# Three programs between attention stages made one, and score tiles of the third cross stage sent in whole pairs

## Chip, cores and metric
The kernel runs on one core of a Trainium2 chip. The metric is the device time of one execution in microseconds (us), the median of several runs; lower is better.

## What is computed
A transformer of four layers over x of 8 batches x 256 tokens x 128 channels (16 heads of 8), with a context of 8 x 1601 tokens and one conditioning vector per batch. Layers 0 to 2 have the same outline; the norms, gates and score masks differ:

```
mod = act(cond) @ W_mod + b_mod                    # shift, scale, gate per batch
h = norm(x) * (1 + scale) + shift
x = x + gate * proj(self_attention(q, k, v of h))    # 256 keys; layer 1 rotary, layer 2 windows of 64
x = x + gate * proj(cross_attention(q of h', k and v of ctx))   # 1601 keys; layer 2 keeps the top 16 scores
x = x + gate * mlp(norm(x) * (1 + scale) + shift)    # 128 -> 512 -> 128; layer 2 gated
```

Layer 3 is a cross attention with one head, whose result goes with the normed x into three routed experts and a gate.

## The kernel before, in words
Activations lie transposed, channels on the 128 partitions: `p.x` and `p.o_all` hold 2048 tokens as columns, worked on in NC = 4 chunks of CH = 512 columns. Queries and keys are split in three bf16 parts each (so products keep float32's precision), written to DRAM (`store_q`, `store_k`, three DMAs each, runs of 1 KB) and read back per batch in stacked form (`q_st`, `k_st`; two DMAs each, runs of 512 B).

Each stage is a `nc.Block()` of its own: five programs (TensorE PE, VectorE DVE, ScalarE ACT, GpSimd POOL, SyncE SP, which issues all DMAs), with a barrier at its end. `program` calls, for each layer, `stage_load` (weights and vectors by DMA, then the modulation: 6 or 9 matmuls, `p.modv`), `stage_project` (`Norm`, then keys, queries and values; splits by VectorE and GpSimd; stores), `stage_attention` self (in whose tail `Onward` makes the cross queries), `stage_attention` cross and `stage_mlp` (`OutProj`, `Norm`, up and down matmuls). Layer 2's cross attention is `stage_last`, which has mixed into it the layer's MLP, and layer 3's attention; then come `stage_load(3)` and `stage_experts`.

`Norm` goes breadth first: mean of all four chunks, then variance, then a matmul that spreads 1/std (`diag`), then scale and shift on ScalarE. `stage_mlp` uses two PSUM banks for up (L1463) and one for down (L1450); after the last residual (L1492 or L1490, and L1496) the block ends. `stage_load` then loads the weights (L189). `stage_project` makes the projections (L556) and values (L564), splits (L596 to L608), and stores queries and keys (L157, L164) and values (L532) in the order q0 k0 q1 k1 q2 q3 v v k2 v v k3. In the self attention SP first loads masks (layer 2 only, L1029, L1030), then queries, keys and values of batches 0 and 1 (L1036, L1043, L1048); after a zero matmul (L1133) the first score (L1156) waits for the keys.

Within attention stages a planner (`Plan`) sets a fixed order. A step k is one tile of 128 keys of one unit n (a unit is a batch b and a group of 4 heads, 32 in all; 13 steps per unit in cross attention, NT = 13). In each step TensorE makes `x_scores(k)`, items of the ring of PSUM banks, and `values` for a step before. The ring carries score tiles ("s": 128 queries of one head x about 400 keys; NS = 32 tiles per unit), turned maxima ("m"), projections of the next batch's context ("k", "v") and in `stage_last` the side items of `LastOrder` (co, mean, var, bc, m1a, m1b, m2, q3, k3, v3, s3, t3, x3, rb at steps counted from `first(b)`, here called d). How many score tiles have been sent by the end of step k is

```
upto = min(NU * self.NS + (turn if beside else 0), ((k + 1) * self.NS // NT + lead) // 2 * 2)
```

In `stage_last` (BANKS = 3, four rows `s_sb` of 1601 scores) ScalarE copies each score tile to `s_sb` (L2004). One such row holds a head's scores of 128 queries, 4 tiles; a pair is two of them, 8 tiles. VectorE finds the 16 largest of each row in 8 operations per pair (MAX8, MATCH_REPLACE8, L2283 to L2292), which are counted in `g["chain"]`, 8 per pair just as the tiles. Before its row can be filled with the scores of two pairs later, ScalarE makes `un` of it (`mark`, L1995), which `x_scores` uses to leave out all but the 16 largest. VectorE's side work for step k (`between(k)`: co and m2 L2214, mean L2219, var L2221, bc L2223, m1b L2227, s3 L2230) is put in the chain at

```
def slot(k):
    return (k + 1) * NS // NT + LEAD - 10        # LEAD = HQ * NCH + 16 = 48
```

Of the kernel before, what the change touches and what calls it, by code (L numbers as in the profile page):

```python
# [7 lines left out]
F32 = mybir.dt.float32  # L8
# [96 lines left out]
class Program:  # L105
    def __init__(self, nc, ctx, io):
# [12 lines left out]
        self.vec = self.sb("vec", [P, V_MAX])  # L119
        self.modv = self.sb("modv", [P, 9, B])  # L120
# [5 lines left out]
        self.v_dram = dram("v_dram", (B, P, 2, NH * VW), F32)  # L126
# [44 lines left out]
def vector(p, layer, name, n=0):  # L171
    at = V_OFF[layer][0][name] + n
    return p.vec[:, at:at + 1]


def stage_load(p, layer):

    nc, (w_off, n_w), (v_off, n_v) = p.nc, W_OFF[layer], V_OFF[layer]
    loaded, act_ready, mm_ready, mod_ready, rows_set = (p.sig(s) for s in ("w_loaded", "cact_ready", "mod_mm", "mod_ready", "rows_set"))
    n_mod = dict(L_WEIGHTS[layer]).get("mod", 0)  # L180
    n_dma = 2 + (5 if layer == 0 else 0)
    scale_slots = [] if layer == 3 else [m[layer][0] for m in (MOD_SELF, MOD_CROSS, MOD_MLP) if m[layer][0] is not None]
    with ExitStack() as ctx:
        mod_ps = p.ps(f"mod_ps{layer}", [P, 9, B], ctx)
        block = ctx.enter_context(nc.Block())

        @block.sync
        def _(sp):
            sp.dma_start(p.w[:, 0:n_w, :], p.io[f"w{layer}"]).then_inc(loaded.sem, 16)  # L189
            sp.dma_start(p.vec[:, 0:n_v], p.io[f"v{layer}"]).then_inc(loaded.sem, 16)  # L190
            if layer == 0:
                sp.dma_start(p.cond[:], p.io["cond"]).then_inc(loaded.sem, 16)
                sp.dma_start(p.const[:], p.io["const"]).then_inc(loaded.sem, 16)
                sp.dma_start(p.neg_id[:], p.io["neg_id"]).then_inc(loaded.sem, 16)
                sp.dma_start(p.id_bf[:], p.io["id_bf"]).then_inc(loaded.sem, 16)
                sp.dma_start(p.x[:], p.io["x"]).then_inc(loaded.sem, 16)
            sp.wait_ge(loaded.sem, loaded.at(16 * n_dma))

        if layer == 0:
            @block.gpsimd  # L200
            def _(pool):
                for hf in range(2):
                    nc.gpsimd.memset(p.q_st[64 * hf + 32:64 * hf + 64], 0.0).then_inc(rows_set.sem, 1)
                pool.wait_ge(rows_set.sem, rows_set.at(2))

        if n_mod:
            @block.scalar
            def _(act):
                act.wait_ge(loaded.sem, loaded.at(16 * n_dma))

                nc.scalar.activation(p.cact[:], p.cond[:], ACT.Copy if layer == 1 else ACT.Silu).then_inc(act_ready.sem, 1)

            @block.tensor
            def _(pe):
                pe.wait_ge(loaded.sem, loaded.at(16 * n_dma))
                pe.wait_ge(act_ready.sem, act_ready.at(1))
                for s in range(n_mod):
                    last = nc.tensor.matmul(mod_ps[:, s, :], weight(p, layer, "mod", s), p.cact[:], start=True, stop=True)
                last.then_inc(mm_ready.sem, 1)

            @block.vector
            def _(dve):
                if layer == 0:
                    for hf in range(2):
                        nc.vector.memset(p.k_flat[64 * hf + 32:64 * hf + 64], -1.0)
                dve.wait_ge(mm_ready.sem, mm_ready.at(1))
                bias = p.vec[:, v_off["mod"]:v_off["mod"] + n_mod]
                nc.vector.tensor_tensor(p.modv[:, 0:n_mod, :], mod_ps[:, 0:n_mod, :],
                                        bias[:, :, None].to_broadcast([P, n_mod, B]), ALU.add).then_inc(mod_ready.sem, 1)
                dve.wait_ge(mod_ready.sem, mod_ready.at(1))  # L230
                for s in scale_slots:
                    last = nc.vector.tensor_scalar(p.modv[:, s, :], p.modv[:, s, :], 1.0, None, ALU.add)
                last.then_inc(mod_ready.sem, 1)
    loaded.passed(16 * n_dma)
    if n_mod:
        act_ready.passed(1)
        mm_ready.passed(1)
        mod_ready.passed(2)
# [96 lines left out]
class Norm:  # L335
# [4 lines left out]


    def __init__(self, p, ctx, layer, scale, shift):
        self.p, self.layer, self.scale, self.shift = p, layer, scale, shift
        self.xc = p.sb("n_xc", [P, NC, CH], F32, ctx)
        self.sq = p.sb("n_sq", [P, NC, CH], F32, ctx)
        self.diag = p.sb("n_diag", [P, NC, CH], F32, ctx)
        self.h = p.sb("n_h", [P, NC, CH], F32, ctx)
        self.rv = p.sb("n_rv", [P, NC, 4], F32, ctx)
        self.rstd = p.sb("n_rstd", [P, NC, 4], F32, ctx)
        self.mean_ps = p.ps("n_mean", [P, NC, CH], ctx)  # L350
        self.var_ps = self.mean_ps[:, :, 0:4]
# [73 lines left out]
def mod_slot(p, layer, slot):  # L425
    if slot is None:
        return lambda b: None
# [2149 lines left out]
```

## Time and profile before

| | |
|---|---|
| three runs, median (lowest to highest) | 4625.27 us (4620.71 to 4640.73) |
| the profiled execution, its time | 4624.74 us |
| its span, first to last instruction | 4623.0 us |
| PE busy | 3625.3 us, 78% |
| PEld (weight loads) busy | 1609.1 us, 35% |
| DVE busy | 3536.7 us, 77% |
| ACT busy | 2945.9 us, 64% |
| POOL busy | 691.4 us, 15% |
| moved by DMA | 280.05 MB |
| mean granted TensorE clock | 0.80 |

Times in the profile are us from the span's start. A row of the timeline gives start, duration, engine, line, operation, output and inputs, how many instructions were merged, and in brackets the idle time of the engine before it with what ended it. In a row of windows the numbers in brackets are instructions. The order of the engines in a row of windows is PE, PEld, DVE, ACT, POOL. A DMA share can come out a little above 1. In front of a row with SPq the engine only issues; the transfer comes after.

### The profile page before, as it was taken

The numbers are of one execution on the slowest core, as the hardware profiler recorded it, in microseconds if no ns is written. First come the engines' busy times: TensorE is split into PE (matmuls) and PEld (weight loads), VectorE is DVE, ScalarE is ACT, GpSimd is POOL, SyncE is SP. The second block draws the span as 40 slices with busy tenths as digits, with TensorE's granted clock in tenths as the row PEclk, the third lists the DMA queues.
The fourth block names the chain that finished last, engine by engine and source line by source line (L and its number), as shares of the span: only waits on it lengthen the run. The fifth ranks groups of instructions, "written<-read, shape, count | busy, mean of one in ns | idle before, by whom it ended". The sixth has DMA issues, their size and how long they took to land. (4 is left out here: it accounts for less than half of the span.)

```text
span 4623.0 us, 75349 instructions
## 1 busy us (share of the span) xinstructions
PE 3625.3 (78%) x28388; PEld 1609.1 (35%) x28388; DVE 3536.7 (77%) x5424; ACT 2945.9 (64%) x5480; POOL 691.4 (15%) x1464
## 2 busy tenths in 40 slices
PE   2769999976789999858367778787787878778877
PEld 2323333332323333323132334334343434334543
DVE  7658989826568888537699998898989889898213
ACT  1556888844647878627377776767677677766413
POOL 1322122004234242013011010000101000000000
PEclk7788999987879999878666677777777667766769
DMA  4553353205434333144311011110111011000000
GB/s 138 147 132 85 85 112 84 57 22 144 120 91 95 90 94 80 24 107 118 80 36 43 22 29 37 31 34 19 40 30 37 18 32 34 13 12 10 13 19 9
DMA packets 277795, 280.05 MB, mean 61 GB/s; under 512 B 38960, under 2 KB 252472, under 8 KB 276536
## 3 DMA queue, kind: packets, MB, share of 16 engines
q1 hardware_dynamic: 277432, 275.22, 23.9%
q8 instruction: 226, 3.70, 0.4%
q14 instruction: 137, 1.12, 0.1%
HBM read 149.53 MB, written 124.43 MB: 59 GB/s over the span
## 5 line engine op out<-in xcount | busy, mean ns | idle before, releaser
L1369 DVE TENSOR_REDUCE mpart<-ring 128x1 f32<-128x400 f32 (+2 forms) x2816 | 1293.0, 524 | 273.9 <-PE ring L1156 267.1
L1287 ACT ACTIVATE prob<-xa_ps 128x512 f32<-128x512 f32 (+1 forms) x2048 | 1109.8, 596 | 243.5 <-PE xa_ps L1201 223.1
L2068 ACT ACTIVATE prob<-x_ps 128x512 f32<-128x512 f32 (+1 forms) x832 | 451.9, 598 | 313.3 <-PE x_ps L1926 246.5
L1156 PE MATMUL ring<-k_st,q_st 52*128 52x400 bf16 (+2 forms) x2560 | 580.7, 340 | 43.2 <-DMA k_st<-k_dram 11.3
L1790 PE MATMUL ring<-k_st,q_st 52*128 52x400 bf16 (+1 forms) x1024 | 330.5, 444 | 294.2 <-ACT s_sb L2004 276.3
L1220 PE MATMUL xa_ps<-prob,va 128*9 128x256 f32 x6656 | 506.4, 383 | 0.4 <-ACT prob L1287 0.4
L2283 DVE MAX8 mpart<-s_sb 128x8 f32<-128x1601 f32 x256 | 456.1, 1817 | 61.5 <-ACT s_sb L2004 61.5
L2004 ACT ACTIVATE s_sb<-ring 128x400 f32<-128x400 f32 (+1 forms) x1024 | 468.2, 517 | 40.1 <-PE ring L1790 31.8
L1995 ACT ACTIVATE un<-s_sb 128x1601 fp8e4<-128x1601 f32 x256 | 392.9, 1536 | 128.8 <-DVE s_sb L2292 128.3
L2286 DVE MATCH_REPLACE8 s_sb<-mpart,s_sb 128x1601 f32<-128x1601 f32 x256 | 461.9, 1812 | 0.0
L2292 DVE MATCH_REPLACE8 s_sb<-m8b,s_sb 128x1601 f32<-128x1601 f32 x256 | 461.8, 1812 | 0.0
L2289 DVE MAX8 m8b<-s_sb 128x8 f32<-128x1601 f32 x256 | 454.6, 1816 | 0.0
L1201 PE MATMUL xa_ps<-q_st,k_st 55*128 55x256 bf16 (+1 forms) x3840 | 408.6, 279 | 56.7 <-ACT prob L1287 43.5
L1921 PE MATMUL x_ps<-neg_id,un 128*128 128x128 bf16 (+1 forms) x3328 | 349.9, 268 | 47.0 <-ACT prob L2068 46.1
L1921 PEld LDWEIGHTS x_ps<-neg_id,un 128*128 128x128 fp8e4 (+1 forms) x3328 | 286.3, 128 | 188.6 <-ACT prob L2068 131.0
L1943 PE MATMUL av_ps<-prob,va 128*9 128x256 f32 (+1 forms) x3328 | 338.2, 496 | 0.0
L1156 PEld LDWEIGHTS ring<-k_st,q_st 52*128 52x128 bf16 x2560 | 180.1, 95 | 408.5 <-DVE mpart L1369 259.6
L1790 PEld LDWEIGHTS ring<-k_st,q_st 52*128 52x128 bf16 x1024 | 84.8, 112 | 511.8 <-ACT s_sb L2004 387.3
L1201 PEld LDWEIGHTS xa_ps<-q_st,k_st 55*128 55x128 bf16 (+1 forms) x3840 | 142.3, 96 | 314.1 <-ACT prob L1287 287.4
L1926 PE MATMUL x_ps<-q_st,k_st 55*128 55x256 bf16 (+1 forms) x1664 | 210.1, 342 | 0.0
L1271 ACT ACTIVATE mT<-ring 24x128 bf16<-24x128 bf16 x160 | 41.9, 262 | 211.9 <-PE ring L1162 210.3
L1220 PEld LDWEIGHTS xa_ps<-prob,va 128*9 128x9 f32 x6656 | 105.3, 88 | 188.8 <-issue 108.2
(291 smaller groups left out, 4195.3 us busy)
## 6 DMA issues: line engine op xcount, KB each, us to landing
k_st<-kc_dram SPq DMA_DIRECT2D x192, 300.2 KB, 5.5
o_dram<-o_sb SPq DMA_DIRECT2D x192, 128.0 KB, 1.8
kc_dram<-k SPq DMA_DIRECT2D x72, 300.0 KB, 3.4
ctx_t<-in_ctxT SPq DMA_DIRECT2D x24, 800.5 KB, 4.8
q_st<-q_dram SPq DMA_DIRECT2D x80, 192.0 KB, 4.2
kc_dram<-k SPq DMA_DIRECT2D x72, 200.0 KB, 3.9
k_st<-k_dram SPq DMA_DIRECT2D x48, 192.0 KB, 5.0
kc_dram<-k SPq DMA_DIRECT2D x24, 300.8 KB, 3.3
```

What stands on the lines that cost most here:

```text
L1156: nc.tensor.matmul(ring_ps[:, r % BANKS, 0:w], q_st[rows, b % NQ, 2 * t + pl, qt * P:(qt + 1) * P], k_st[rows, slot_of(n), pl, c0:c0 + w], ...
L1201: last = nc.tensor.matmul(x_ps[0:sizes[j], (2 * s + hf) % XBANKS, pl * T:(pl + 1) * T], k_st[rows, slot_of(n), pl, keys], q_st[rows, b % N ...
L1220: last = nc.tensor.matmul(av_ps[32 * k:32 * k + VW, n % 2, :], va[0:sizes[j], b % NVB, j, G * t + k, :], prob[0:sizes[j], s % NPROB, (2 * ...
L1287: nc.scalar.activation(prob[0:size, s % NPROB, hf * 512:(hf + 1) * 512], x_ps[0:size, (2 * s + hf) % XBANKS, :], ACT.Exp, scale=HEAD_SCALE ...
L1369: nc.vector.tensor_reduce(mpart[:, n % 4, row, c:c + 1], ring_ps[:, r % BANKS, 0:chunks[c][1]], AX.X, ALU.max).then_inc(g["red"].sem, 1)
L1921: nc.tensor.matmul(x_ps[0:sizes[j], (2 * s + hf) % XBANKS, pq * P:(pq + 1) * P], un[:, n % 2, hf * G + pq, keys], p.neg_id[:], start=pq == ...
L2004: nc.scalar.activation(s_sb[:, q % 4, c0:c0 + w], ring_ps[:, r % BANKS, 0:w], ACT.Copy).then_inc(g["rout"].sem, 1)
L2068: nc.scalar.activation(prob[0:size, s % NPROB, hf * 512:(hf + 1) * 512], x_ps[0:size, (2 * s + hf) % XBANKS, :], ACT.Exp, scale=HEAD_SCALE ...
L2283: ins = nc.vector.max(best, sc)
L2286: ins = nc.vector.match_replace(sc, best, sc, -BIG)
L2289: ins = nc.vector.max(m8b[:, half, :], sc)
L2292: ins = nc.vector.match_replace(sc, m8b[:, half, :], sc, -BIG)
```

## The change
- `stage_load` is called once, for layer 0. `stage_project` and `stage_mlp`, with `OutProj` and `Norm`, are replaced by `stage_between` (class `Between`), called ahead of each self attention: for layer 0 with norm and projections alone, for layers 1 and 2 from the output projection of the cross attention before through the MLP to the new layer's projections, in one block.
- Its SP program loads the next layer's weights up to the place of `co` at the start, the rest after the last down matmul. `p.vec` and `p.modv` have two sets. Next modulation: matmuls between norm and up.
- PSUM use is a rotation of four banks for all products and four for statistics.
- Values go straight to SBUF (`vs`) and stay for all batches; `v_dram` goes, and so do the loads of values.
- Queries and keys of batches 0 and 1 are loaded within the stage, in front of its last three stores; layer 2's masks at its start. The order of stores is q0 k0 q1 k1 q2, loads, q3 k2 k3.
- In `Plan`, with `beside` (only `stage_last`), the number of tiles sent is rounded down to whole pairs, 8; LEAD is 52; VectorE's side work goes behind the second operation of the last pair sent.
- The one zero matmul of 512 columns in `stage_last` becomes two of 256.

```diff
-def stage_load(p, layer):
+def stage_load(p):
...
-            sp.dma_start(p.w[:, 0:n_w, :], p.io[f"w{layer}"]).then_inc(loaded.sem, 16)
+            sp.dma_start(p.w[:, 0:W_OFF[0][1], :], p.io["w0"]).then_inc(loaded.sem, 16)
...
+class Between:
...
+    HEAD = ("op", "mean", "var", "diag", "norm", "mod", "up", "down")
+    TAIL = ("mean", "var", "diag", "norm", "proj")
+    NF = 4
...
+        self.by_pool = [("k", c) for c in range(NC - 1)]
+        self.by_dve = [("q", c) for c in range(NC)] + [("k", NC - 1)]
...
+    def out(self, use):
+        return self.bank[:, self.at[use] % 4, :]
...
+        def bank_free(use):
+            u = self.at[use]
+            if u == 3 and self.layer is not None:
+                pe.wait_ge(s["bias"].sem, s["bias"].at(1))
+            if u >= 4:
+                old = self.uses[u - 4]
+                read = s[self.reader(old)]
+                pe.wait_ge(read.sem, read.at(self.nth[old]))
...
+            elif k == "mod" and c == 0:
+                pe.wait_ge(s["w"].sem, s["w"].at(32))
+                bank_free(("mod", 0))
+                act_in = p.cond if self.nxt == 1 else p.cact
+                for i in range(self.n_mod):
+                    last = nc.tensor.matmul(self.out(("mod", 0))[:, i * B:(i + 1) * B], weight(p, self.nxt, "mod", i), act_in[:], start=True, stop=True)
+                last.then_inc(s["mm"].sem, 1)
+            elif k == "up":
+                pe.wait_ge(s["h"].sem, s["h"].at(2 * n + 2))
+                for f in range(self.NF):
+                    use = (("up", f), c)
+                    bank_free(use)
+                    nc.tensor.matmul(self.out(use), weight(p, self.layer, "m1", f), self.h[:, c, :], start=True, stop=True).then_inc(s["mm"].sem, 1)
+            elif k == "down":
+                pe.wait_ge(s["act"].sem, s["act"].at(self.nth[("up", self.NF - 1), c]))
+                bank_free(("down", c))
+                for f in range(self.NF):
+                    last = nc.tensor.matmul(self.out(("down", c)), weight(p, self.layer, "m2", f), self.hid[:, c, f, :], start=f == 0, stop=f == self.NF - 1)
+                last.then_inc(s["mm"].sem, 1)
...
+            elif k == "proj":
+                pe.wait_ge(s["h"].sem, s["h"].at(2 * n + 2))
+                for name in self.names:
+                    use = (name, c)
+                    bank_free(use)
+                    if name == "v":
+                        for i in range(4):
+                            last = nc.tensor.matmul(self.out(use)[:, i * P:(i + 1) * P], self.h[:, c, i * P:(i + 1) * P], weight(p, self.nxt, "v"), start=True, stop=True)
+                    else:
+                        last = nc.tensor.matmul(self.out(use), weight(p, self.nxt, name), self.h[:, c, :], start=True, stop=True)
+                    last.then_inc(s["mm"].sem, 1)
+
...
+                    if name == "v":
+                        if c == 0:
+                            act.wait_ge(s["ones"].sem, s["ones"].at(1))
+                        dst = self.vs[:, 2 * c:2 * c + 2].rearrange("p b j h w -> p (b j) h w")[:, :, :, 0:HD]
+                        nc.scalar.activation(dst, self.out(use).rearrange("p (k h d) -> p k h d", k=4, d=HD), ACT.Copy).then_inc(s["act"].sem, 1)
+                        continue
...
+            if k in ("op", "down"):
+                self.residual(dve, c, k)
...
+            elif k == "proj" and c == 0:
+                for what, chunk in self.by_dve:
+                    done = self.split(dve, nc.vector, s["dchain"], done, what, chunk, s["dparts"])
+
...
+    def pool(self, pool):
+        self.p.nc.gpsimd.memset(self.vs[:], 1.0).then_inc(self.s["ones"].sem, 1)
+        done = 0
+        for what, c in self.by_pool:
+            done = self.split(pool, self.p.nc.gpsimd, self.s["pchain"], done, what, c, self.s["pparts"])
...
+        p, s, nxt = self.p, self.s, self.nxt
+        if self.layer is not None:
+            n_w, free = W_OFF[nxt][1], W_OFF[self.layer][0]["co"]
+            sp.dma_start(p.w[:, 0:free, :], p.io[f"w{nxt}"][:, 0:free, :]).then_inc(s["w"].sem, 16)
+            sp.dma_start(p.vec[:, nxt % 2, 0:V_OFF[nxt][1]], p.io[f"v{nxt}"]).then_inc(s["w"].sem, 16)
+        if self.rope:
+            sp.dma_start(self.table[:], p.io["rope"][:, :, 0:T]).then_inc(s["tab"].sem, 16)
+        if nxt == 2:
+            for hf in range(2):
+                rows = slice(64 * hf + STACK, 64 * hf + STACK + MASK_ROWS)
+                for par in range(NQ):
+                    sp.dma_start(self.q_self[rows, par], p.io["qmask"][:, None, :].to_broadcast([MASK_ROWS, NH // 2, T])).then_inc(s["init"].sem, 16)
+                keys = p.k_flat[rows, 0:NQ * NH // 2 * T].rearrange("r (n c) -> r n c", c=T)
+                sp.dma_start(keys, p.io["kmask"][:, None, :].to_broadcast([MASK_ROWS, NQ * NH // 2, T])).then_inc(s["init"].sem, 16)
+        if self.layer is not None:
+            sp.wait_ge(s["mm"].sem, s["mm"].at(self.at["down", NC - 1] + 1))
+            sp.dma_start(p.w[:, free:n_w, :], p.io[f"w{nxt}"][:, free:n_w, :]).then_inc(s["w2"].sem, 16)
+
+        def store(what, c):
+            mine, ready = (self.by_pool, s["pparts"]) if (what, c) in self.by_pool else (self.by_dve, s["dparts"])
+            sp.wait_ge(ready.sem, ready.at(mine.index((what, c)) + 1))
+            cols, st = slice(c * CH, (c + 1) * CH), s["st" if c else "st0"]
+            if what == "q":
+                store_q(sp, p.q_dram, cols, self.parts[:, c, 0], st)
+            else:
+                store_k(sp, p.k_dram, cols, self.parts[:, c, 1], st)
+
+        for what, c in (("q", 0), ("k", 0), ("q", 1), ("k", 1), ("q", 2)):
+            store(what, c)
+        sp.wait_ge(s["st0"].sem, s["st0"].at(32 * len(RUNS)))
+        for b in range(Q_AHEAD):
+            load_queries(p, sp, self.q_self, b, s["loaded"])
+            load_keys(p, sp, b, s["loaded"])
+        for what, c in (("q", 3), ("k", 2), ("k", 3)):
+            store(what, c)
+        for name in ("loaded", "st", "w", "w2", "init"):
+            if self.totals[name]:
+                sp.wait_ge(s[name].sem, s[name].at(self.totals[name]))
...
-        self.ring, self.items = [], {}
+        self.ring, self.items, self.upto = [], {}, {}
+        whole = 2 * NCH if beside else 2
         self.at, self.nth, self.n_act, self.n_dve = {}, {}, 0, 0
...
-            upto = min(NU * self.NS + (turn if beside else 0), ((k + 1) * self.NS // NT + lead) // 2 * 2)
+            self.upto[k] = upto = min(NU * self.NS + (turn if beside else 0), ((k + 1) * self.NS // NT + lead) // whole * whole)
...
-        va = p.va if cross else p.sb("va_self", [P, NVB, NT, NH, VW], F32, ctx)
+        va, NVB = (p.va, 2) if cross else (vs, B)
...
-            for b in bload_at.get(-1, []):
-                load_q(b)
-                load_k_self(b)
-                load_v(b)
...
-    LEAD = HQ * NCH + 16
+    LEAD = HQ * NCH + 20
...
-            nc.tensor.matmul(av_ps[:].rearrange("p u c -> p (u c)"), zero[:, 0:P], zero[:], start=True, stop=True)
+            for u in range(2):
+                nc.tensor.matmul(av_ps[:, u, :], zero[:, 0:P], zero[:], start=True, stop=True)
...
-                return (k + 1) * NS // NT + LEAD - 10
+                return plan.upto[k] - 2 * NCH + 2
...
-            stage_load(p, layer)
-            if layer == 0:
-                stage_context_norm(p)
-            stage_project(p, layer)
-            stage_attention(p, layer, "self")
+            with ExitStack() as mid:
+                vs = p.sb("vs", [P, B, 2, NH, VW], F32, mid)
+                q_self = p.sb("q_masked", [P, NQ, NH // 2, T], BF16, mid) if layer == 2 else p.q_st
+                stage_between(p, layer - 1 if layer else None, layer, vs, q_self)
+                stage_attention(p, layer, "self", vs, q_self)
             if layer < 2:
                 stage_attention(p, layer, "cross")
-                stage_mlp(p, layer)
         with ExitStack() as last:
             nx = p.sb("nx3", [P, TOK], F32, last)
             stage_last(p, nx)
-            stage_load(p, 3)
+            stage_load_last(p)
```

## Rows read from the trace of the kernel before

**Rows 1.** Timeline, layer 0 to 1 (start us, us, engine, line, operation, [idle before])
```profile
965.02 0.69 DVE L474 TENSOR_TENSOR x<-x,op_res 128x512 f32<-128x512 f32 x1
...
978.12 1.88 PE L1463 MATMUL ml_ps<-n_h,w 128*128 128x512 f32 x4
...
1006.85 3.67 PE L1450 MATMUL ml_ps<-ml_hid,w 128*128 128x512 f32 x8 [1.26 <-DVE ml_res L1492]
...
1011.66 0.69 DVE L1496 TENSOR_TENSOR x<-x,ml_res 128x512 f32<-128x512 f32 x1
...
1039.93 14.10 PE L556 MATMUL pj_ps<-n_h,w 128*128 128x512 f32 x32
...
1044.47 3.43 DVE L596 TENSOR_TENSOR pj_f<-pj_f,pj_table 128x512 f32<-128x512 f32 x2 [3.65 <-ACT pj_f L576]
...
1080.43 0.69 DVE L608 TENSOR_TENSOR pj_q<-pj_f,pj_q 128x512 bf16<-128x512 f32 x1
...
1095.46 0.61 PE L1156 MATMUL ring<-k_st,q_st 52*128 52x256 bf16 x4 [5.65 <-DMA k_st<-k_dram]
```

**Rows 2.** Timeline, layer 1 to 2
```profile
1962.13 1.88 PE L1463 MATMUL ml_ps<-n_h,w 128*128 128x512 f32 x4
...
2006.16 3.98 PE L218 MATMUL mod_ps<-cact,w 128*128 128x8 f32 x18 [10.08 <-ACT cact L211]
...
2026.48 7.39 PE L556 MATMUL pj_ps<-n_h,w 128*128 128x512 f32 x16
...
2034.13 1.58 SPq L157 DMA_DIRECT2D q_dram<-pj_q  x3
...
2057.59 1.32 SPq L1029 DMA_DIRECT2D q_masked<-in_qmask  x4
...
2073.79 0.61 PE L1156 MATMUL ring<-k_st,q_masked 52*128 52x256 bf16 x4 [15.15 <-DMA k_st<-k_dram]
```

**Rows 3.** Timeline, projections of layer 0 to its first score
```profile
136.37 1.56 SPq L157 DMA_DIRECT2D q_dram<-pj_q  x3
...
160.56 0.60 PE L1133 MATMUL xa_ps<-zero 1*128 1x512 bf16 x1 [20.88 <-DVE zero L1357]
...
166.84 0.61 PE L1156 MATMUL ring<-k_st,q_st 52*128 52x256 bf16 x4 [5.68 <-DMA k_st<-k_dram]
```

**Rows 4.** Timeline of VectorE, first two pairs of the third cross stage
```profile
2252.50 3.56 DVE L2283 MAX8 mpart<-s_sb 128x8 f32<-128x1601 f32 x2 [3.27 <-ACT s_sb L2004]
...
2266.60 3.55 DVE L2283 MAX8 mpart<-s_sb 128x8 f32<-128x1601 f32 x2
```

**Rows 5.** Window before side work starts: us, busy per engine, PEclk, DMA share, GB/s
```profile
2300.00:2600.00 300.00, 205.85 (x1543) 89.12 (x1545) 300.00 (x258) 213.37 (x368) 26.95 (x52) 0.67 0.13 36
```

**Rows 6.** Waits of VectorE, 2250 to 4290 us (us in total, times, longest)
```profile
DVE mpart L2283 <- ACT s_sb L2004: 61.5, 15, 10.4
...
DVE ls_res L2214 <- PE ring L1837: 35.7, 12, 6.5
...
DVE ls_xc L2223 <- PE ring L1837: 14.5, 11, 1.6
...
DVE ls_xc L2219 <- PE ring L1837: 13.9, 8, 2.5
...
DVE ls_mpart L2230 <- PE ring L1853: 13.0, 14, 1.7
...
DVE ls_rv L2221 <- PE ring L1844: 10.8, 7, 1.7
```

**Rows 7.** Windows: layer 0's stores, then its loads
```profile
148.00:152.00 4.00, 0.00 (x0) 0.00 (x0) 1.98 (x4) 0.00 (x0) 0.00 (x0) 0.50 1.02 349
...
164.00:166.00 2.00, 0.00 (x0) 0.00 (x0) 0.00 (x0) 0.00 (x0) 0.00 (x0) 0.50 1.19 190
```

**Rows 8.** Page, costliest groups: ScalarE's copies of scores and its marks
```profile
L2004 ACT ACTIVATE s_sb<-ring 128x400 f32<-128x400 f32 (+1 forms) x1024 | 468.2, 517 | 40.1 <-PE ring L1790 31.8
...
L1995 ACT ACTIVATE un<-s_sb 128x1601 fp8e4<-128x1601 f32 x256 | 392.9, 1536 | 128.8 <-DVE s_sb L2292 128.3
```

More of the change, by code:

```diff
@@ L197, in _ @@
-            sp.wait_ge(loaded.sem, loaded.at(16 * n_dma))
[L199 to L233, printed above, removed]
@@ new lines, in _ @@
+        @block.tensor
+        def _(pe):
+            pe.wait_ge(loaded.sem, loaded.at(16 * n_dma))
+            pe.wait_ge(act_ready.sem, act_ready.at(1))
+            for s in range(n_mod):
+                last = nc.tensor.matmul(mod_ps[:, s, :], weight(p, 0, "mod", s), p.cact[:], start=True, stop=True)
+            last.then_inc(mm_ready.sem, 1)
+        @block.vector
+        def _(dve):
+            for hf in range(2):
+                nc.vector.memset(p.k_flat[64 * hf + 32:64 * hf + 64], -1.0)
+            dve.wait_ge(mm_ready.sem, mm_ready.at(1))
+            bias = p.vec[:, 0, at:at + n_mod]
+            nc.vector.tensor_tensor(modv[:, 0:n_mod, :], mod_ps[:, 0:n_mod, :], bias[:, :, None].to_broadcast([P, n_mod, B]), ALU.add).then_inc(mod_ready.sem, 1)
+            dve.wait_ge(mod_ready.sem, mod_ready.at(1))
+            for s in scale_slots(0):
+                last = nc.vector.tensor_scalar(modv[:, s, :], modv[:, s, :], 1.0, None, ALU.add)
+            last.then_inc(mod_ready.sem, 1)
@@ L539, in _ @@
-            store_v(2)
-            store_v(3)
-            store("k", 3)
-            sp.wait_ge(stored.sem, stored.at(16 * len(RUNS) * NI))
-            sp.wait_ge(v_st.sem, v_st.at(32 * NV))
+            bt.sp(sp)
         @block.tensor
         def _(pe):
-            norm.pe(pe)
-            for i in range(NI):
-                what, c = items[i]
-                names = names_of[what]
-                norm.wait_h(pe, c)
-                for r in range(stepn):
-                    n = i * stepn + r
-                    if n >= 3:
-                        pe.wait_ge(pf.sem, pf.at(n - 2))
-                    nc.tensor.matmul(pp[:, n % 3, :], weight(p, layer, names[r]), norm.h[:, c, :], start=True, stop=True).then_inc(proj.sem, 1)
@@ L557, in _ @@
-            for g in range(NV):
-                m = NI * stepn + g
-                if g < 3:
-                    pe.wait_ge(pf.sem, pf.at(m - 2))
-                else:
-                    pe.wait_ge(v_out.sem, v_out.at(g - 2))
-                for k in range(4):
-                    last = nc.tensor.matmul(pp[:, m % 3, k * P:(k + 1) * P], norm.h[:, g, k * P:(k + 1) * P], weight(p, layer, "v"), start=True, stop=True)
-                last.then_inc(v_mm.sem, 1)
+            bt.pe(pe)
         @block.scalar
@@ L627, in stage_project @@
[L627 to L632 removed]
+            bt.pool(pool)
+    bt.done()
 class Onward:
@@ L900, in by_step, with stage_attention @@
     return out
-def stage_attention(p, layer, kind):
+def stage_attention(p, layer, kind, vs=None, q_self=None):
     nc = p.nc
     cross = kind == "cross"
-    masked = layer == 2 and not cross
     rope = layer == 1
```

641 lines of the change are left out of this document (272 added, 369 removed).

## The prediction

> **What bounds the kernel now.** I read the page first. VectorE is busy for 77% of the span, TensorE for 78% and ScalarE for 64%; no engine is full throughout, so the stages have to be taken one by one. The chain that ended last reaches back only into the experts' stage, which the change leaves alone. I then read the timeline around the three places where `stage_project` hands over to a self attention, and for the third cross stage (2247 to 4467 us) the waits and busy times of VectorE.
>
> At the hand-over between layers 0 and 1 every step is serial [rows 1]. The last residual ends at 1011.66 + 0.69 = 1012.35. Only behind it, in a program of its own, are the weights asked for and the modulation made; then the norm runs, and projection matmuls start at 1039.93. The first split of queries starts at 1044.47 and the first score at 1095.46. Layer 1 to 2 has the same shape [rows 2]. At the start of layer 0 [rows 3] only the last part is there: first store 136.37, first score 166.84.
>
> In the third cross stage VectorE's top-16 passes are the metronome: one pair of score rows (eight operations) takes 2266.60 - 2252.50 = 14.10 us [rows 4], so 128 pairs need 1805 us. They last to about 4292. Up to 2600 VectorE never idles [rows 5], but after that, once the side work of the last layer (`LastOrder`) is mixed in, it waits; the largest kinds of wait are [rows 6], 149 us together.
>
> **The change part by part, the hand-overs.**
> The order of the levels (op, mean, var, diag, norm, up, down) is what `OutProj`, `Norm` and `stage_mlp` do now, so I cost everything up to the norm at nothing. From there, layer 0 to 1:
> - The modulation's matmuls are put ahead of the MLP. 18 of them take 3.98 us [rows 2], 12 then 2.65. Their weights are asked for at the start of the stage, some 20 us earlier, and MLP work covers that.
> - Up and down are 64 TensorE instructions over 512 columns. 32 of that kind took 14.10 us [rows 1], so 64 take 28.2. Four banks in place of two take out the bank waits.
> - The last residual ends 1.8 us after the last down matmul (1012.35 - 1010.52) [rows 1].
> - The next norm: from the end of a first-half residual to the first matmul behind the norm it is 978.12 - 965.71 = 12.4 us [rows 1].
> Start of the projections: 978.12 + 2.65 + 28.2 + 1.8 + 12.4 = 1023.2 against 1039.93, a gain of 16.8. For layer 1 to 2: 1962.13 + 3.98 + 28.2 + 1.8 + 12.4 = 2008.5 against 2026.48, a gain of 18.0.
>
> From projections to scores. The 8 stores of values and the 2 loads go; queries and keys of two batches are loaded before the last three stores. This looks like much, but the DMA engines carry it. In the stores the rate is 349 GB/s, in the loads with their half as long runs 190 GB/s [rows 7]. The 24 stores of queries and keys write 6.3 MB, 18.2 us, and the 8 loads fetch 1.57 MB, 8.3 us: 26.5 us of transfers. From a first store at 136.37, with 0.7 to get going, that ends at 163.6. Now it is 7.5 MB of stores, 21.4 us, to 158.5, and the zero matmul behind the barrier ends at 161.16 [rows 3], 2.7 later. So the first score comes at 166.3 against 166.84: a gain of 0.5. The stores of values (1.18 MB, 3.4 us) are what is saved, and putting the loads ahead is worth little, because they queue on the same engines.
> If instead SP's issue were the limit, the last store would leave about 1.6 us sooner than now and the loads would cost nothing afterwards: 7 us. I take 0.5, because the share of the DMA engines in [rows 7] is full; 7 is the other end.
> The Trainium skill (DMA: Bandwidth & Descriptors, Specifications) puts line rate at runs of 512 B and up, which is just what these loads have. By that rule the loads would take 4.5 us and each hand-over would gain 3.8 us more; the trace disagrees, 190 against 349 GB/s.
>
> Layer 1 to 2 gains the same, and the masks: they are loaded ahead of the stage's work instead of between barrier and score. Now it is 2073.79 - 2034.13 = 39.7 us from the first store to the first score [rows 2]; afterwards 166.3 - 136.4 = 29.9. Gain 9.8 in all. In layer 1 the rope splits set the pace, 51.0 us from the first split to the score [rows 1]. VectorE's five splits end at 1081.12, 36.7 us in. The loads have then been at the DMA engines since the third, so the last three stores (2.36 MB, 6.8 us) run from about 39 us on, and 2.7 follow: 48.5. Gain 2.5.
> Sum: 0.5 + 16.8 + 2.5 + 18.0 + 9.8 = **48 us** (47.6). The low end is 32 (TensorE enters the MLP or the norm at the low clock, which doubles its part of a few microseconds, and the stores and loads mix badly), the high end adds 3 x 6.5: 67.
>
> **The change part by part, whole pairs.** The score tiles of a pair are now sent in one step every 3.25 steps, and VectorE reads the side results of a step behind the second operation of the last pair sent. Sending a pair needs the pair two before it to be finished, because there are four rows of `s_sb`. I count in chain operations of 1.76 us how far VectorE has gone past that point when it asks for a side result. Now it is 0 to 6: co, mean, var and the first m1b have 0 or 1, bc 2, m2 3. Afterwards it is 10 for each, 17.6 us instead of 0 to 10.6. So the waits for mean, bc, var and s3 in [rows 6] should go: 13.9 + 14.5 + 10.8 + 13.0 = **52 us**. I keep the wait for ls_res (35.7): most of it is the co at the end of the heavy stretch. The m1b waits stay also: step d+13 gets the same slot as bc of d+10, and shift, m1 and Silu must run between the two.
>
> The heavy stretch (x3 and values3, 13 steps) is limited by TensorE and ScalarE; 61.5 us of waits on s_sb are of there [rows 6]. Whole pairs give some 4 us more lead per batch, 7 x 4 = 28 us saved; against that the eight copies at 517 ns and two marks at 1536 ns [rows 8] come in one lump in which TensorE has little to do. I take these two as equal: 0. Ends: all of 61.5 + 35.7 goes (-97), or as much is added (+97).
> At the end the last batch but one's m1b is read behind the chain instead of inside it, and m2 waits for it: about one step, 14.1 / 3.25 = 4 us lost.
> Sum: 52 - 4 = **48 us**. The rest (LEAD 16 to 20, two zero matmuls for one, the second set of vectors) I cost at nothing: the stage's first burst is 48 tiles before and after.
>
> The profiled execution is 4623.0 + 1.7 around it = 4624.7, as good as the median 4625.3. Forecast: 4624.7 - 48 - 48 = **4529 us**.
>
> **The rivals.**
> 1. *The stage swallows it.* The side results come in time but VectorE waits for s_sb instead, since the round of TensorE and ScalarE is the true limit once side work is mixed in. For it: the s_sb waits are the largest single kind. Against: VectorE is full until 2600. The hand-overs' 48 alone: 4577.
> 2. *The heavy stretch is relieved as well.* The longer lead is enough. 4529 - 97 = 4432, halfway 4480.
> 3. *Slower.* Place: `x_scores` and `values` in the steps behind a lump. During eight copies and two marks (8 x 0.517 + 2 x 1.536 = 7.2 us) TensorE has eight short matmuls. The granted clock in the quiet stretch is 0.67 [rows 5], a mixture of the two levels, 1.2 and 2.4 GHz. If it fell to 0.50 throughout, its busy share of 206/300 would be 0.69 x 0.67 / 0.50 = 0.92, that is 13.0 of a pair's 14.1 us, and with 1.6 to 3.1 us of lump that TensorE can't fill 14.6 to 16.1. It decides from 48/128 = 0.4 us a pair. At 1.2 us a pair over 128 pairs, 154 us: 4577 + 154 = 4731. Against: a busier TensorE has the clock given back, and VectorE waits now in spite of small lumps, so the present order isn't better at that either.
> The Trainium skill (TensorE: Matmul & The Clock Gate, HAM oscillation) says that matmul groups with idle gaps between them are throttled again each time; that is this rival, and it would give its 4731.
> 4. *The hand-overs don't give 48*, for example because waves in one program run at the low clock or the final wait on stores hides the earlier start: 25 instead, with 48 from the stage: 4552.
>
> **How the numbers follow.** Forecast (4495 to 4560) 0.45, rival 1 0.18, rival 2 0.17, rival 3 0.12, rival 4 0.08. Under about 0.5%, 23 us, a measurement can't tell the two kernels apart. Faster by more: everything but rival 3 and a part of rival 1, 0.85; within: 0.06; slower: 0.09, since a small loss of clock would only eat the gain. The range goes from 4440, most of rival 2, to 4600, the hand-overs' 32 with 7 lost in the stage; it leaves out rival 3 and the far end of rival 2, under 2 in 10.
>
> **What would show it.** In the profile after, no weight load between the MLP and the norm; projections some 17 and 18 us sooner after the cross stage's end; first score 29 to 31 us after the first store in layers 0 and 2, with the DMA share full in between. If that is 23 us, the DMA argument is wrong. In the third stage VectorE's waits for mean, bc, var and s3 near zero, the m1b waits still there, pairs still 14.1 us apart before side work starts. If they are over 14.5 us there, or the granted clock is near 0.5, rival 3 holds; if the wait for s_sb grows by as much as the others shrink, rival 1.

## The result and the profile after

Three runs of the changed kernel took 4751.39 us (4739.22 to 4765.99) against 4625.27: a ratio of **1.0266**, 95% interval 1.0207 to 1.0326. It is **slower by about 126 us**, where 4529 was forecast. The profiled execution took 4739.22 us, its span is 4737.4, against 4623.0: 114.4 more. VectorE and ScalarE are busy as long as before: 3539.4 us (3536.7) and 2948.6 (2945.9). TensorE is busy for 3714.6 us against 3625.3, 89 more; in one stretch the same work runs at a lower clock, as shown below. Ratios here and below compare fast executions alone; one slower execution each of e6, e9 and e12 is in the median but not in the ratio.

**The hand-overs.** The timeline of after, with the rows that answer to [rows 1 to 3]:

```profile
138.19 1.56 SPq L156 DMA_DIRECT2D q_dram<-bt_parts  x3
...
169.10 0.61 PE L1217 MATMUL ring<-k_st,q_st 52*128 52x256 bf16 x4
...
969.75 0.69 DVE L569 TENSOR_TENSOR x<-x,bt_f 128x512 f32<-128x512 f32 x1
...
983.15 1.40 PE L456 MATMUL bt_bank<-cond,w 128*128 128x8 f32 x12
...
984.41 13.98 PE L463 MATMUL bt_bank<-bt_h,w 128*128 128x512 f32 x32
...
998.23 13.90 PE L468 MATMUL bt_bank<-bt_hid,w 128*128 128x512 f32 x32
...
1013.19 0.69 DVE L569 TENSOR_TENSOR x<-x,bt_f 128x512 f32<-128x512 f32 x1
...
1025.33 3.60 PE L479 MATMUL bt_bank<-bt_h,w 128*128 128x512 f32 x8
...
1078.37 0.61 PE L1217 MATMUL ring<-k_st,q_st 52*128 52x256 bf16 x4
...
1933.89 0.69 DVE L569 TENSOR_TENSOR x<-x,bt_f 128x512 f32<-128x512 f32 x1
...
1990.96 1.88 PE L479 MATMUL bt_bank<-bt_h,w 128*128 128x512 f32 x4
...
1998.60 1.58 SPq L156 DMA_DIRECT2D q_dram<-bt_parts  x3
...
2028.91 0.61 PE L1217 MATMUL ring<-k_st,q_masked 52*128 52x256 bf16 x4
```

The norm no longer waits for weights or modulation: the rest of the next layer's weights is asked for at 1012.15, beside it, and nothing there waits for them. The first score comes 17.1 us sooner in layer 1 (1095.46 - 1078.37) and 44.9 in layer 2 (2073.79 - 2028.91), but 2.3 later in layer 0. Between layer 0's stores and its first score, from 147 to 166 us, the share of the DMA engines is 1.00 to 1.25, full throughout.

**The third cross stage.** I take the starts of VectorE's 128 pairs (first MAX8 of each). The first is at 2213.1 us instead of 2252.5, 39.4 sooner; the last at 4384.7 instead of 4276.0. From first to last it is 2171.6 us instead of 2023.5, 148.1 more, and 352.7 instead of 347.0 from there to the end. -39.4 + 148.1 + 5.7 = 114.4: the whole difference.

The 148.1 are not spread evenly. The first 26 pairs are 14.1 us apart in both kernels, and the granted clock there is no lower than before: 0.69 (2260 to 2560 us) against 0.67 in [rows 5]. After that a batch of 16 pairs takes (mean of five batches, in groups of four pairs) 61.9, 62.5, **71.2**, 67.6 us before and 62.6, 64.4, **90.4**, 70.5 after. The third group is the heavy stretch, with x3 and values3; six of them hold 114 of the 148 us. Two heavy groups of before, then two of after (columns as in [rows 5]):

```profile
3104.60:3173.65 69.05, 59.07 (x429) 33.12 (x425) 57.38 (x53) 47.75 (x87) 2.87 (x7) 0.83 0.10 26
3624.93:3699.75 74.82, 68.48 (x415) 37.59 (x413) 57.47 (x52) 45.35 (x83) 2.85 (x7) 0.66 0.09 24
```

```profile
2807.34:2901.66 94.32, 80.43 (x418) 42.62 (x419) 57.41 (x51) 45.69 (x86) 2.25 (x6) 0.59 0.07 19
3097.98:3187.36 89.38, 74.34 (x418) 40.10 (x419) 57.40 (x50) 45.56 (x86) 2.25 (x6) 0.65 0.08 20
```

VectorE has 57.4 us of work in each. TensorE's work, counted at full speed as busy time by clock, is about the same in both kernels: 59.07 x 0.83 = 49 and 68.48 x 0.66 = 45 before, 80.43 x 0.59 = 47 and 74.34 x 0.65 = 48 after. What grew is its busy time, at a lower clock, and its idle time, from 6 to 10 us to 14 to 15. I call a lump what now comes in one step: eight score tiles, with their copies and two marks on ScalarE. One lump in that stretch (timeline of after, without weight loads):

```profile
2844.44 0.54 PE L1747 MATMUL ring<-k_st,q_st 52*128 52x401 bf16 x2
2844.68 1.08 ACT L2025 ACTIVATE prob<-x_ps 128x512 f32<-128x512 f32 x2 [0.97 <-PE x_ps L1883]
2844.92 1.04 PE L1900 MATMUL av_ps<-prob,va 65*9 65x256 f32 x8
2845.89 0.51 PE L1747 MATMUL ring<-k_st,q_st 52*128 52x400 bf16 x1
...
2846.31 1.53 ACT L1952 ACTIVATE un<-s_sb 128x1601 fp8e4<-128x1601 f32 x1
...
2848.27 1.53 ACT L1952 ACTIVATE un<-s_sb 128x1601 fp8e4<-128x1601 f32 x1
2848.44 0.51 PE L1747 MATMUL ring<-k_st,q_st 52*128 52x400 bf16 x1 [2.04 <-ACT s_sb L1961]
2849.84 2.88 ACT L1961 ACTIVATE s_sb<-ring 128x401 f32<-128x401 f32 x7
2850.40 1.70 PE L1747 MATMUL ring<-k_st,q_st 52*128 52x400 bf16 x4 [1.45 <-ACT s_sb L1961]
...
2852.36 1.83 DVE L2240 MAX8 mpart<-s_sb 128x8 f32<-128x1601 f32 x1 [9.45 <-ACT s_sb L1961]
```

TensorE fills the three banks of the ring with three tiles and then stands behind ScalarE's two marks, 2.04 and 1.45 us. VectorE waits 9.45 us for the lump: it has used up its lead. The clock ahead of it, from the lump before on, and around it (windows of after, 4 us each):

```profile
2819.00:2823.00 4.00, 3.46 (x38) 1.82 (x37) 2.52 (x3) 1.88 (x4) 0.00 (x0) 1.00 0.00 0
2823.00:2827.00 4.00, 0.78 (x3) 0.24 (x3) 0.00 (x0) 3.94 (x6) 0.00 (x0) 0.85 0.00 0
...
2839.00:2843.00 4.00, 4.00 (x17) 2.10 (x18) 3.91 (x5) 1.08 (x2) 0.00 (x0) 0.50 0.45 72
2843.00:2847.00 4.00, 3.40 (x25) 1.36 (x24) 0.00 (x0) 2.44 (x5) 0.00 (x0) 0.50 0.00 0
2847.00:2851.00 4.00, 1.11 (x3) 0.30 (x3) 0.00 (x0) 3.94 (x6) 0.00 (x0) 0.50 0.10 33
2851.00:2855.00 4.00, 4.00 (x11) 2.12 (x11) 2.64 (x2) 1.72 (x5) 0.00 (x0) 0.50 0.00 0
```

The clock is at full speed until the lump at 2823, in which TensorE is busy for 0.78 of 4 us. From 2827 to 2887 every such window shows 0.50, the level of 1.2 GHz, though TensorE is hardly ever idle between two lumps (from 2827 to 2843 it is busy for 4.00 of every 4 us). The waits of VectorE from 2213 to 4386 us, for [rows 6]:

```profile
DVE mpart L2240 <- ACT s_sb L1961: 166.1, 38, 9.4
DVE ls_res L2171 <- PE ring L1794: 70.2, 7, 14.6
DVE ls_xc L2176 <- PE ring L1794: 30.4, 7, 4.8
DVE ls_hid L2184 <- ACT ls_hid L1970: 28.3, 6, 4.9
DVE ls_rv L2178 <- PE ring L1801: 12.9, 7, 2.2
DVE ls_mpart L2187 <- PE ring L1810: 10.7, 8, 1.7
```

Only the wait for bc (L2180) went, 14.5 us. Those for co and m2 (`ls_res`, L2171) and for the mean (L2176) doubled, so did that of m1b for ScalarE (L2184, 14.8 before), and the wait for score rows grew from 61.5 to 166.1. All VectorE's waits in the stage add up to 320 us, against 173 before: this is the 148 us.

### The profile page after: what moved, and what is told of

It is laid out like the page before. It is cut to its first block and busy times, and to the rows that moved or that the text cites. A ratio compares the mean times of both kernels' runs of the same rounds, so it can differ in the third digit from the quotient of the medians.

```text
span 4737.4 us, 75209 instructions
## 1 busy us (share of the span) xinstructions
PE 3714.6 (78%) x28389; PEld 1638.1 (35%) x28389; DVE 3539.4 (75%) x5424; ACT 2948.6 (62%) x5477; POOL 692.2 (15%) x1464
## 5 line engine op out<-in xcount | busy, mean ns | idle before, releaser
L1747 PE MATMUL ring<-k_st,q_st 52*128 52x400 bf16 (+1 forms) x1024 | 366.6, 443 | 489.3 <-ACT s_sb L1961 483.4
L2240 DVE MAX8 mpart<-s_sb 128x8 f32<-128x1601 f32 x256 | 454.3, 1816 | 166.2 <-ACT s_sb L1961 166.1
L1961 ACT ACTIVATE s_sb<-ring 128x400 f32<-128x400 f32 (+1 forms) x1024 | 433.4, 526 | 16.2 <-PE ring L1747 8.2
L1900 PE MATMUL av_ps<-prob,va 128*9 128x256 f32 (+1 forms) x3328 | 318.9, 471 | 0.0
L1986 ACT ACTIVATE ls_hid<-ring 128x256 f32<-128x256 f32 (+1 forms) x104 | 39.9, 383 | 238.8 <-PE e_ps L1838 228.9
```

The source lines that it names most:

```text
L1747: nc.tensor.matmul(ring_ps[:, r % BANKS, 0:w], q_st[rows, b % NQ, 2 * t + pl, qt * P:(qt + 1) * P], k_st[rows, t, pl, c0:c0 + w], start=Tr ...
L2240: ins = nc.vector.max(best, sc)
```

## The experiments

All ratios are against the kernel before, run on the same chip beside each. "Twos" means tiles sent in twos, as before.

### e1, e2: which half of the change costs

```diff
-        whole = 2 * NCH if beside else 2
+        whole = 2
-    LEAD = HQ * NCH + 20
+    LEAD = HQ * NCH + 16
-                return plan.upto[k] - 2 * NCH + 2
+                return (k + 1) * NS // NT + LEAD - 10
```

> The kernel after with the third cross stage's plan as before: tiles sent in twos, LEAD 16, VectorE's side work at the old slots. If the merged stages keep what the trace of after shows (third cross stage entered at 2208.3 instead of 2247.6, 39.3 us sooner) and all of the loss is the whole pairs: 4625 - 39 = 4586. If the merged stages themselves disturb the later stage (longer gaps, another state of the clock), it stays above 4600.

4569.55 us, ratio 0.9865 (0.9839 to 0.9891), 16 us better than expected. In its profiled execution, the fastest of six (4543.20), the third cross stage is 2002.8 us from first to last pair, against 2023.5 in before with the same plan: executions differ by that much in this stage. For e2 the kernel before got these three places as they are in after.

> The kernel before with only the plan of the third cross stage changed: whole pairs, LEAD 20, side work behind the second operation of the last pair sent. From the two traces the stage grew by 145 us from first to last pair and by 9 behind it: 4625 + 154 = 4779. If the loss needs both changes, it is nearer to 4625.

4818.04 us, ratio 1.0400 (1.0381 to 1.0418). **The merged stages gain, and all of the loss is the plan of the third cross stage**; it costs about 4% here and 1.0266 / 0.9865 = 4.1% behind the merged stages. In the profile of e2 five heavy groups take 94.3 us at clock 0.59, and the last takes 95.1. e2 is 39 us above its expectation; in after four of the six ran at 0.65 in 89.4 us, with the same instructions, which explains some 20 of them.

### e3, e11, e10: the late slots

```diff
-        whole = 2 * NCH if beside else 2
+        whole = 2
```

> The kernel after with score tiles sent in twos again, but with LEAD 20 and VectorE's side work as late as in after (6 operations before the last tile sent). Theory lump (eight copies and two marks in one step leave TensorE idle and keep its clock low in the 13 steps of x3 and values3): the loss goes, and since the side results come in time the waits of VectorE for mean, bc, var and s3 go as well: 4586 or up to 30 below. Theory slot (ScalarE and TensorE stand behind results that VectorE reads later than before): the loss stays, 4700 or more.

4552.17 us, ratio 0.9821 (0.9800 to 0.9841); theory slot falls. Theory lump stands, though it is 34 us below 4586 where I had allowed 30. The waits of VectorE in the stage, in e3:

```profile
DVE mpart L2240 <- ACT s_sb L1961: 114.2, 42, 6.7
DVE ls_res L2171 <- issue: 13.3, 4, 6.0
DVE ls_rv L2178 <- PE ring L1801: 6.3, 5, 1.6
DVE ls_hid L2184 <- PE ring L1794: 3.3, 6, 0.8
```

Here the waits for mean, bc and s3 are gone. But the wait for score rows is 114.2 us; in e1 it is 45.0, in before 61.5. From first to last pair e3 takes 1984.2 us, 18.6 less than e1, but 360.2 from the last pair to the end, where e1 takes 348.2: 12 of the 18.6 us are lost again.

> Twos with late slots once more, beside the run before: 0.982 again (4552). It shows whether the 0.4% over hand-overs only stand.

4555.73 us, ratio 0.9859 (0.9836 to 0.9883): the 0.4% over e1 does not stand. The late slots together with the longer lead are worth between 0.1 and 0.4%, by the two runs, within the noise of e1.

```diff
-        whole = 2 * NCH if beside else 2
+        whole = 2
-                return plan.upto[k] - 2 * NCH + 2
+                return (k + 1) * NS // NT + LEAD - 10
```

> The kernel after with twos and LEAD 20, and VectorE's side work at the old formula, so that it is asked for 4 operations later than with LEAD 16 (hand-overs only, ratio 0.9865) and 4 earlier than with late slots (0.9821). If the later slots are what gained, it lies between, at 0.984 (4560), with VectorE's waits for mean, bc, s3 and var at about half of 50 us. If the longer lead alone gained, it is at 0.982; if VectorE's wait for s_sb swallows all of it, at 0.9865.

4599.81 us, ratio 0.9952 (0.9935 to 0.9970). A miss: it lies outside both ends. Its heavy groups take 78.2 us at clock 0.67, those of e3 70 to 76 at 0.66 to 0.76. So with LEAD 20 in both, the late slots are worth 0.9 to 1.3%, and the longer lead with the old formula costs 0.9% against e1. Why this spacing is worse stays open.

### e5, e6, e7: the size and the place of the lumps

```diff
-        whole = 2 * NCH if beside else 2
+        whole = NCH if beside else 2
```

> The kernel after with tiles sent in fours (half a pair: ScalarE's two marks come with every other lump, and a lump is 4 or 0 copies with the marks, 4 without). Theory lump: TensorE's gap is in the lump with the marks and shrinks by the four copies that are now in another step (4 x 0.4 us = 1.6 of 4.5 us), the clock comes back more often: between twos with late slots (4552) and whole pairs (4739 to 4751), about 4640. If only a lump as long as a whole pair hurts: 4560. If any late slot with more than two tiles hurts alike: 4730.

4712.06 us, ratio 1.0160 (1.0128 to 1.0192). The middle I expected is wrong: a heavy group takes 90.15 us at clock 0.64, as long as with whole pairs. Four tiles with the marks are already more than the ring's three banks take; that this is the reason was not tried by itself.

For e6 and e7 the size depends on the step (e7 has 8 and 2 exchanged), and `upto` never falls below what was sent:

```diff
-            self.upto[k] = upto = min(NU * self.NS + (turn if beside else 0), ((k + 1) * self.NS // NT + lead) // whole * whole)
+            dense = k >= 111 and ((k - 20) % 52 >= 39 or (k - 20) % 52 < 2)
+            whole = 2 if not beside else 2 if dense else 8
+            self.upto[k] = upto = max(sent, min(NU * self.NS + (turn if beside else 0), ((k + 1) * self.NS // NT + lead) // whole * whole))
```

> The kernel after, with twos in the steps from the first x3 to two behind the last of each batch (15 of 52) and whole pairs in the others. Between after (4751) and twos everywhere (4552) lie 199 us. By the pair times of after the groups of four pairs in which x3 and values3 run hold about 20 of the 26 us lost per batch, so theory lump in the heavy stretch gives 4552 + 50 = 4600. If the loss were spread over all steps by their number, twos in 29% of them would give back 58: 4690.

4604.60 us, ratio 0.9917 (0.9888 to 0.9947); the heavy groups take 73.4 us.

> The counterpart: whole pairs only in those 15 steps, twos in the others. Theory lump in the heavy stretch: 4552 + 6 x 20 = 4670 or somewhat more. If the loss is spread by steps: 4552 + 58 = 4610. The two experiments together should add up to the whole difference of 199 us if the parts are independent.

4635.49 us, ratio 0.9997 (0.9983 to 1.0011); the heavy groups take 84.1 to 90.3 us. So 15 of 52 steps alone cost 1.4 to 1.8% against twos (e11, e3). But the parts don't add up: with 0.9821 for twos, 0.96% (e6) and 1.76% (e7) make 2.7 of the 4.5% between twos and after. The profiles say the same, from first to last pair: e6 takes 52 us more than e3, e7 82 more, after 187 more. Lumps outside the heavy stretch cost more when there are lumps inside as well: the four pairs behind it take 61 to 62 us in e3, 61.0 in e7 (lumps inside alone), 64.0 in e6 (outside alone) and 70.7 in after.

### e4, e9, e12: the clock

TensorE's gaps in a lump are filled with matmuls that nobody reads, into a bank of `x_ps` that the next `x_scores` overwrites. FILL is 14 in e4 and 24 in e9 and e12; `step[0]` is the step in hand.

```diff
+                if i % 8 in (3, 4) and 0 <= step[0] < END - 1:
+                    if i % 8 == 3:
+                        pe.wait_ge(g["exp"].sem, g["exp"].at(2 * step[0] + 1))
+                    for _ in range(FILL):
+                        nc.tensor.matmul(x_ps[:, (2 * step[0] + 2) % XBANKS, 0:P], p.id_bf[:], p.neg_id[:], start=True, stop=True, skip_group_check=True)
                 ring_free(r)
```

> The kernel after, and in each lump 14 more matmuls of 128 columns ahead of its 4th tile and 14 ahead of its 5th, where TensorE waits for ScalarE's marks (they write a bank of x_ps that the next x_scores overwrites). They fill about 3 of the 4.5 us that TensorE idles per lump. If the granted clock stays at 0.50 in the 13 steps of x3 because of these gaps, it returns to 1.00 in a part of them and a batch's 13 steps take about 75 instead of 89 us: some 7 x 14 = 100 us less, 4650. If the gaps have nothing to do with the clock, nothing is won: 4739 or up to 30 more, since the added matmuls delay tiles at the low clock.

4702.93 us, ratio 1.0151 (1.0134 to 1.0168): 1.1% less than after. The clock rose to 0.72, but the groups fell only from 89.4 to 87.3 us.

> As the kernel with 14 matmuls at each of the two places of a lump, with 24 at each. With 14 the granted clock in the 13 heavy steps was 0.72 to 0.73 instead of 0.59 to 0.65, TensorE was still idle for 8.5 us in a group of four pairs, and the group took 87.3 us. If low clock and gaps hang together, the filled gaps bring 0.85 or more and the group to about 75 us (48 us of useful matmuls at full clock and 4 x 6.5 us of lumps): some 60 us less than with 14, 4640. If the clock does not follow the gaps, it stays near 0.7, the further matmuls delay the tiles at the low clock, and it takes 4710 to 4740.

4569.48 us, ratio 0.9868 (0.9840 to 0.9895). **10 more idle matmuls at each of two places gave 2.8%** (2.4% by e12, on e4's chip). The waits that come with them are the same in e4, so they are not what gains.

> The same kernel as before, for the profile of an undisturbed execution: 4569 again, 0.987 of before. If the gain of 170 us over whole pairs without filling is the clock's, the heavy steps show a granted clock of 0.95 or more and a group of four pairs takes about 70 to 75 us; the lumps' own price, against twos, is what is then left of the 16 us a group.

4589.91 us, ratio 0.9913 (0.9883 to 0.9942). Heavy groups of e12, three from one execution (4574.77 us, one of its faster) with the same instructions:

```profile
2778.74:2847.39 68.65, 63.79 (x618) 40.08 (x619) 57.40 (x50) 46.12 (x86) 2.25 (x6) 1.00 0.09 26
3284.48:3365.27 80.79, 76.84 (x619) 47.64 (x619) 57.40 (x50) 46.32 (x86) 2.25 (x6) 0.81 0.09 22
3550.51:3636.54 86.03, 81.18 (x610) 48.23 (x611) 57.40 (x50) 45.70 (x85) 2.25 (x6) 0.76 0.08 21
```

68.65 us at 1.00, 80.79 at 0.81, 86.03 at 0.76. With whole pairs and full clock a heavy group takes less than the 71.2 us of before. **The low clock is what makes the lumps expensive**: without it nothing is left of the 19 us a group, though twos gain from a higher clock as well (e13). That the clock stays up for a whole group is not assured by 24: the expectation of 0.95 or more holds for two of the six groups, and the later ones of the same execution fell back. What the matmuls supply is also not separated: they shorten TensorE's gaps, and they give it more work altogether.

### e13, e14: the same lever without lumps

Twos with late slots as in e3, and ahead of every second tile FILL matmuls (8, then 16), behind a wait for the exps two halves earlier.

```diff
+                if i % 2 == 0 and 1 <= step[0] < END - 1:
+                    pe.wait_ge(g["exp"].sem, g["exp"].at(2 * step[0]))
+                    for _ in range(FILL):
+                        nc.tensor.matmul(x_ps[:, (2 * step[0] + 2) % XBANKS, 0:P], p.id_bf[:], p.neg_id[:], start=True, stop=True, skip_group_check=True)
                 ring_free(r)
```

> Twos with late slots (ratios 0.9821 and 0.9859), and ahead of every second score tile 8 matmuls of 128 columns into a bank of x_ps, some 32 per pair of rows. If the clock is what limits the heavy steps with twos as well: there TensorE's own work is 48 us for four pairs at full clock, with the added ones 55, less than VectorE's 57, so a group falls from 74 to about 60 us, 7 x 14 = 98 us less: 4460. If the clock does not follow, the added matmuls cost 8 x 0.107 us x 16 = 14 us a group: 4650.

4512.94 us, ratio **0.9758** (0.9721 to 0.9795), faster than both kernels. Heavy groups of e3 and of e13:

```profile
3310.78:3381.99 71.21, 64.13 (x407) 35.88 (x404) 57.39 (x51) 43.07 (x82) 2.25 (x6) 0.71 0.09 25
```

```profile
3035.53:3099.51 63.98, 59.50 (x544) 36.32 (x542) 57.29 (x51) 45.13 (x84) 2.26 (x6) 0.95 0.11 28
```

Four of e13's six groups take 64 us at 0.95, the first and the last 73 and 78. So of the 98 us I had expected 29 to 47 came, by the ratios of e3 and e11. At nearly full clock a group of twos takes 64.0 us and one of whole pairs 68.7: some 5 us is the lump's own price, as an estimate, since the two have different numbers of idle matmuls.

> The same with 16. If the clock is held at full speed: 48 + 16 x 16 x 0.053 = 62 us a group, 4480; that is better than with 8 only if 8 don't hold it. If the clock does not follow: 4750.

4521.33 us, ratio 0.9775 (0.9737 to 0.9812), not to be told from e13. Its heavy groups show 0.97 to 1.00 and take 63 to 66 us: now steady, but TensorE is busy there for 97% of the time.

### e8: the place of the loads in the hand-over

With twos as in e3:

```diff
-        for what, c in (("q", 0), ("k", 0), ("q", 1), ("k", 1), ("q", 2)):
+        for what, c in (("q", 0), ("k", 0), ("q", 1), ("k", 1), ("q", 2), ("q", 3), ("k", 2), ("k", 3)):
...
-        for what, c in (("q", 3), ("k", 2), ("k", 3)):
-            store(what, c)
```

> Twos with late slots (4552), and in the merged stages the loads of queries and keys of batches 0 and 1 behind all 24 stores instead of ahead of the last nine. If the DMA engines carry the time between first store and first score, as the prediction has it, the order changes nothing: 30 to 31 us from first store to first score in layer 0, as in after (30.9), and the time is the same within 10 us. If the loads ahead of the last stores hide something, the first score comes up to 8 us later in each of three layers: 4575.

4559.50 us, ratio 0.9832 (0.9806 to 0.9859), within the two runs of twos. In layer 0 of e8 the first store is issued at 139.82 us, and then (timeline):

```profile
161.04 0.99 SPq L683 DMA_DIRECT2D k_st<-k_dram  x2
...
170.06 0.61 PE L1215 MATMUL ring<-k_st,q_st 52*128 52x256 bf16 x4
```

30.2 us from first store to first score, 30.9 in after and 29.8 in e3; in layer 2 it is 30.8, 30.3 and 30.4. There the order doesn't matter, as expected if the DMA engines carry the time. In layer 1, where the splits set the pace, it does: 42.4 us (1082.28 - 1039.88) against 38.8 in e3 and 40.2 in e11, too little to show in the whole time.

## Why the prediction was wrong

**The hand-overs (48 forecast, 32 to 67) were right** in every part that the timeline shows. From the end of the last residual of the output projection to the first projection, layer 0 to 1 took 1039.93 - 965.71 = 74.2 us and takes 1025.33 - 970.44 = 54.9: 19.3 gained (16.8 forecast); up and down take 27.9 us (28.2). Layer 1 to 2 took 76.7 and takes 1990.96 - 1934.58 = 56.4: 20.3 (18.0). From projections to first score layer 1 gained 2.5 (2.5) and layer 2 9.4 (9.8), while layer 0 lost 0.4 (+0.5). Sum 51.1 for 47.6. First store to first score is 30.9 us in layer 0 and 30.3 in layer 2 (29.9). Of the 51.1, 44.9 arrive at layer 2's first score: 1.8 were lost before layer 0's first store, and 2.5 and 1.9 in the attention stages of layers 0 and 1, which I can't explain. Those stages are noisy: the third cross stage is entered at 2208.3 in after, 2185.6 in e1 and 2212.2 in e3, with the same code up to there. By e1's ratio the merged stages are worth 50 to 74 us, a little more than the 48 forecast.

**Whole pairs (48 forecast) failed, at two terms.**
- *"Against that the eight copies and two marks come in one lump ... I take these two as equal: 0"*, with ends of -97 and +97. This is the step that failed: the lump's cost was set equal to a saving, without a count of what it does to TensorE. The heavy stretch costs 19 us more per group, 114 in all, beyond my end of +97; the two waits it was made of grew from 97 to 236 us. The end was taken from VectorE's waits of before, but most of what a lump costs comes by TensorE's clock, which this term leaves out.
- *"The waits for mean, bc, var and s3 should go: 52"*. The count of slack holds with twos (e3: only var is left, 6.3). With whole pairs TensorE is itself late, and only bc went, 14.5 of the 52. Even with twos the time isn't won, since VectorE waits for s_sb instead, 114 us for 45 in e1: rival 1's mechanism, which swallowed at least 32 of the 52 us (between e1 and the two runs of twos with late slots lie 0.1 and 0.4%, 3 to 20 us).
- The end of the stage lost 5.7 us, 4 forecast; with twos and the late slots it lost 13 against before (e3).

**Rival 3, 0.12, came true in part.** It gave 4731. But its place was the steps behind every lump, with pairs of 14.6 to 16.1 us from the start, and there nothing happened: 14.1 us for 26 pairs, at a clock of 0.69. It happened where TensorE's busy share was already 59/69 to 68/75, which 4 x 3.5 us of gaps and a clock of 0.59 to 0.65 for 0.66 to 0.83 lift above VectorE's 57 us at once. That the sum fits is chance. My argument against it, *"a busier TensorE has the clock given back"*, is refuted by the windows of 0.50 over 60 us; e4, e9 and e12 show that matmuls put into the gaps bring the clock back. The Trainium skill (TensorE: Matmul & The Clock Gate, HAM oscillation) describes matmul groups that are throttled again by the gaps between them; I named it and gave it 0.12. The trace agrees in part: the clock fell behind the gaps of the lump at 2823. But it then stayed down over several groups and through 16 us in which TensorE was never idle.

Shown, then: the loss is whole pairs (after against e3 and e11, one line changed); most of it is in the heavy stretch; there it is the clock, with an estimated 5 us a group for the lump itself. Open: what in a lump brings the clock down and keeps it down while TensorE is busy, why e10's spacing is worse, and why lumps inside and outside the heavy stretch cost more together.

## What to carry to other kernels

Read the limit of each stretch with the clock beside it: busy time times granted clock is roughly the engine's work at full speed, and a stretch whose TensorE is 92% busy at 0.66 (68.48 of 74.82 us, above) is not full of work but short of clock. Before sending work in larger lumps, look for the engine that must stand still during one; if it is TensorE, the gap can be the smaller part of the price and the clock behind it the larger, as here. And when a wait is removed from the engine at the end of the chain, ask whether what it waits for next comes any sooner.

## What the runs showed that I had not expected

- Matmuls without any use made the kernel faster: 8 of 128 columns ahead of every second score tile, some 3900 in all, took the mean clock from 0.798 (e3) and 0.803 (e11) to 0.862 and the ratio from 0.9821 and 0.9859 to 0.9758.
- The same instructions took 68.65, 80.79 and 86.03 us within one execution, at granted clocks of 1.00, 0.81 and 0.76. And the pattern can repeat from batch to batch: five heavy groups of e2 took 94.3 us, in after one took 94.3 and the next four 89.4.
- Moving 8 loads behind 9 stores changed the time from first store to first score by less than 1 us in layers 0 and 2, where the DMA engines are full, and by 2 to 4 us in layer 1, where they wait for splits (their share in after is 0.51 from 1050 to 1060 us).
